# Norm tiles of x from TensorE transposes to column loads with repeated row numbers, in a cross-attention and FFN kernel

## The chip, the cores and the metric

One core of a Trainium2 chip runs the whole kernel. The metric is the device time in microseconds, the median of three runs. "The profile" is one execution taken by the hardware profiler; times in it count from the start of its span. Engines are PE (TensorE), DVE (VectorE), ACT (ScalarE), POOL (GpSimd) and SP (the engine that issues most DMAs).

## What is computed

```
x: (8, 256, 1024)   ctx: (8, 256, 1024)   32 query heads, 8 key/value heads, width 128
x = x + attention(layernorm(x), ctx, ctx, mask, wq, wk, wv, wo)
x = x + ffn(layernorm(x), qweight, lut4, bias)

layernorm(x) = (x - mean(x)) / sqrt(var(x) + 1e-5)      # over the last axis
attention: q = norm(x) @ wq, k = ctx @ wk, v = ctx @ wv, rotary positions on q and k,
           softmax(q k^T / sqrt(128) + mask) v, then @ wo
ffn:       y = norm(x) @ W^T + bias, W[o, i] = lut4[o, 4-bit code of (o, i)]
```

All arithmetic is float32. Each product is made of three passes over operands that are split in a high and a low part (`PASSES`).

## The kernel before, in words

The program is written out by hand for each engine; a semaphore stands for each hand-over, and each engine works strictly in the order of its own code. There are three stages.

**The key stage** (0 to 390 us of the profile) takes the eight batches one after the other (`batch(b)`, once per engine). On PE a batch is: eight key groups `g` (24 products of 256 columns each, L793) into two PSUM banks in turn, then four value products V0 to V3 (24 products of 512 columns each, L770) into two banks in turn, so that V2 needs the bank that V0 left and V3 the bank that V1 left. A bank is free when ACT has copied its high part and DVE has subtracted the low part (`values_high` L1089, `values_low` L1535). For each key group ACT swaps halves (L996, L997), DVE does cosine, sine and sum (L1372, L1381, L1387) and the low part (L1391), and SP stores it (L536). Between these DVE decodes the FFN weights of one output tile (`decode`, leaves L1568, picks L1575), and at the end it splits the context of the next batch (`context_low`, L1396), which the next batch's first key group needs. PE turns the decoded weights (L751).

**The query stage** (390 to 2160 us) has 256 units `u`, 6.86 us each, in rounds of 16 (`UNITS`): scores (L855), half or all of a query job (L839), attention times values (L896, odd units) and output projection (L925) on PE; mask, reciprocal, 32x32 transposes, splits and residual sums on DVE; exponents on ACT; normalization and query sines on POOL; 64 KB moves of the transposed probabilities on SP and ACT.

**The FFN stage** follows (L965).

**The norm tiles.** The queries need layernorm(x) with the model dimension on the partitions. x has sixteen tiles of 128 rows. Each is loaded with rows on partitions (`load_row`, L436, into `ln_row`), ACT takes the mean (`row_mean`, L1011), centres (`row_center`, L1017) and squares (`row_square`, L1026), DVE makes 1/sqrt (`row_var`, `row_scale`, L1404 to L1414), ACT scales the row (`row_norm`, L1035), PE turns the eight 128x128 blocks into PSUM (`turn_row`, L731, or `turn_side`, L870), ACT and DVE take high and low part out of PSUM into `raw` in two halves (`x_high` L1043, `x_low` L1422), and SP stores them to `x_scratch` (`store_row`, L443). Nine tiles pass in the key stage, in slots given by two tables: K slots (row work during the key groups, turned after V0) and V slots (row work during the values, turned after V3). Seven tiles pass in the query stage, one a round, at `ROW_AT` (u = 8 of a round), turned at u = 13 and 14 (`SIDE`). SP loads x back in `load_turned` (L449).

```
K_ROW = {1: 0, 2: 1, 3: 3, 4: 5, 5: 7, 6: 8}      # batch: tile
V_ROW = {2: 2, 3: 4, 4: 6}
ROW_AT = {UNITS * (e - A_ROWS) + 8: e for e in range(A_ROWS, NT)}
```

Of the kernel before, what the change touches and what calls it, by code (L numbers as in the profile page):

```python
# [14 lines left out]
def build_xattn_ffn(nc, x, ctx, mask, wq, wk, wv, wo, qweight, lut4, bias, x_rows, rope_cos, rope_sin, out):  # L15
# [138 lines left out]
    K_ROW = {1: 0, 2: 1, 3: 3, 4: 5, 5: 7, 6: 8}  # L154
    V_ROW = {2: 2, 3: 4, 4: 6}
# [5 lines left out]
    SIDE = {u + 5 + j: (e, j) for u, e in ROW_AT.items() for j in range(2)}  # L161
# [18 lines left out]
    x_scr = nc.dram_tensor("x_scratch", (NH, 2, C, P, 2, BANK), F32, kind="Internal").ap()  # L180
    res_scr = nc.dram_tensor("residual_scratch", (HT, P, D), F32, kind="Internal").ap()

    with ExitStack() as stack:
# [67 lines left out]
        x_mean, x_var0, x_var1, x_ve, x_sd, x_y, x_e, x_f, x_r = (stat_t[:, 56 + i:57 + i] for i in range(9))  # L251
# [34 lines left out]
        x_stored, res_stored, out_stored = sem("x_stored"), sem("res_stored"), sem("out_stored")  # L286
# [25 lines left out]
        row_ok, x_tr, x_hi, x_lo = sem("row_ok"), sem("x_tr"), sem("x_hi"), sem("x_lo")  # L312
# [45 lines left out]
        def rope_turns(j):  # L358

            return j - 1 if len(JOBS[j]) == 1 and (j == 0 or len(JOBS[j - 1]) == 1) else j  # L360

# [60 lines left out]
        def _(sp):  # L422
# [10 lines left out]
            def load_row(e):  # L433

                sp.wait_ge(x_tr, 2 * e)
                sp.dma_start(ln_row[:, :], x_tiles[e]).then_inc(row_in, 16)  # L436

            def store_row(e, j):

                sp.wait_ge(x_lo, 2 * e + j + 1)  # L440
                dst = x_scr[e // HT, e // REP % 2, 4 * j:4 * j + 4].rearrange("c p l (t n) -> t l p c n", n=P)
                for l in range(2):
                    done = sp.dma_start(dst[e % REP, l], raw_t[:, l * BANK:(l + 1) * BANK]  # L443
                                        .rearrange("p (c n) -> p c n", n=P))
                    done.then_inc(x_stored, 16)
# [58 lines left out]
            def batch(b, first=False, last=False):  # L504
# [14 lines left out]
                if last:  # L519
# [6 lines left out]
                    sp.wait_ge(x_tr, 2 * A_ROWS)  # L526
                    load_piece(wq[2], ln_row[:, :], a_raw_in[1])
                    sp.wait_ge(x_stored, 4 * 16 * A_ROWS)
# [3 lines left out]
                elif b - 1 in V_ROW:  # L532
                    load_row(K_ROW[b])
                for g in range(HKV):
# [13 lines left out]
                    elif not first:  # L548
                        if g == 0 and b - 1 in V_ROW:
                            store_row(V_ROW[b - 1], 0)  # L550
                        if g == TURN_AT[b]:
                            store_weights(b - 1, D0)
                        if g == 3 and b - 1 in V_ROW:
                            store_row(V_ROW[b - 1], 1)
# [27 lines left out]
                if first:  # L582
                    for t in range(TS):
                        load_context(1, t)
                    sp.wait_ge(w_lo, A_SLOTS + 2)
                    load_row(K_ROW[1])
                if b in V_ROW:
                    load_row(V_ROW[b])
                store_values(V0, 0, 0)
                sp.wait_ge(dq_step, b * DQ_STEPS + 1)  # L590
                load_planes(b + 1)
                if b in K_ROW:
                    store_row(K_ROW[b], 0)
                if b not in V_ROW and b in K_ROW and b + 1 in K_ROW:
                    load_row(K_ROW[b + 1])
                store_values(V1, 1, 0)
                if b in K_ROW:
                    store_row(K_ROW[b], 1)
                store_values(V2, 0, 1)
                store_values(V3, 1, 1)  # L600
# [24 lines left out]
            for u in range(NU):  # L625
# [9 lines left out]
                if u + 1 in PIECE and (u + 1) % UNITS not in LOAD_LAST:  # L635
                    if u - 1 in SIDE:
                        sp.wait_ge(x_stored, 4 * 16 * (SIDE[u - 1][0] + 1))
# [20 lines left out]
                if u in SIDE:  # L658
                    store_row(*SIDE[u])
# [4 lines left out]
                for j in range(2):  # L664
                    k = u - (HALF_UNITS - 14 + 8 * j)
                    if k == 1:
                        job = JOB_OF[HALF_UNITS - UNITS + 2 * REP * j + REP - 1]
                        sp.wait_ge(rope_mm, A_ROPES + job + 1)
                    for c in {1: (0, 1), 3: (2, 3), 5: (4, 5), 7: (6, 7)}.get(k, ()):
# [48 lines left out]
        def _(pe):  # L718
# [6 lines left out]

            def turn_row(e):

# [1292 lines left out]
```

## Time and profile before

| | us |
|---|---|
| median of 3 runs (lowest, highest) | 2340.43 (2339.54, 2340.71) |
| the profiled execution's own time | 2341.55 |
| its span | 2339.7 |
| PE busy, share of the span | 2327.5, 99% |
| DVE busy | 1691.2, 72% |
| ACT busy | 1116.5, 48% |
| POOL busy | 568.7, 24% |
| mean DMA rate | 140 GB/s |

Rows of the timeline give start, duration, engine, line, operation, tiles written and read, and in brackets the idle time before it with what ended it. Consecutive instructions of one engine overlap by some 0.1 us in these rows, so starts are used for distances. Rows of the chain of waits give start, duration and what the end of the program hung on. DMA rows give the median time from issue to landing.

### The profile page before, as it was taken

What the parts mean: (1) busy time and instruction counts of PE and PEld (TensorE: products, weight loads), DVE (VectorE), ACT (ScalarE), POOL (GpSimd) and SP (SyncE); (2) the same over time, 40 slices, a digit from 0 to 9 for tenths busy, and PEclk for the clock granted to TensorE, in tenths of its full rate; (3) what the DMA queues carried; (4) which work ended last, traced back from release to release, by engine and by line L of the source; (5) the groups of instructions that cost most, each with busy time, mean ns of one, the idle gap of its engine ahead of it and who ended that gap; (6) DMA issues with size and microseconds to landing.
All of it is one profiled execution on the core that took longest, in us unless ns stands there. A gap on an engine that the chain in (4) does not pass through costs nothing.

```text
span 2339.7 us, 35189 instructions
## 1 busy us (share of the span) xinstructions
PE 2327.5 (99%) x11902; PEld 1989.1 (85%) x11902; DVE 1691.2 (72%) x3811; ACT 1116.5 (48%) x2472; POOL 568.7 (24%) x675
## 2 busy tenths in 40 slices
PE   9999999999999999999999999999999999999999
PEld 8999999888888888888888888888888888888887
DVE  7888777667777777777777767677767776777773
ACT  5555544546464646455544444444444444444110
POOL 1000000332232323232233233323332332331320
PEclk9999999999999999999999999999999999999999
DMA  7466659544344343434456644333433333334442
GB/s 259 155 191 215 203 164 309 159 127 117 113 136 120 110 127 109 131 108 127 112 163 215 204 131 124 93 109 98 126 93 108 107 106 108 91 112 161 148 142 81
DMA packets 330098, 328.26 MB, mean 140 GB/s; under 512 B 32448, under 2 KB 266176, under 8 KB 329920
## 3 DMA queue, kind: packets, MB, share of 16 engines
q1 hardware_dynamic: 294496, 309.88, 43.0%
q10 hardware_dynamic: 35424, 16.14, 2.7%
q8 instruction: 95, 1.56, 0.3%
q14 instruction: 83, 0.68, 0.1%
HBM read 181.73 MB, written 71.30 MB: 108 GB/s over the span
## 4 chain that ended last, share of the span: by engine, by line
PE 94%; DVE 3%; DMA 1%; ACT 1%; issue 1%; POOL 0%; ACTq 0%; SPq 0%; POOLq 0%; DVEq 0%
PE bank L839 29%; PE bank L925 29%; PE bank L855 8%; PE bank L965 7%; PE bank L896 7%; PE bank L793 7%; PE bank L770 5%; DVE residual L1575 1%; DMA x_scratch<-raw 0%; DMA small_split<-probs 0%; POOL probs L1946 0%; DVE residual L1810 0%; DVE residual L1568 0%; PE bank L751 0%; PE bank L870 0%
## 5 line engine op out<-in xcount | busy, mean ns | idle before, releaser
L839 PE MATMUL bank<-acts_split,weights_split 128*128 128x512 f32 (+1 forms) x3192 | 742.9, 382 | 0.0
L925 PE MATMUL bank<-weights_split,small_split 128*128 128x512 f32 x3072 | 741.1, 390 | 1.6 <-DVE small_split L1794 1.6
L925 PEld LDWEIGHTS bank<-weights_split,small_split 128*128 128x128 f32 x3072 | 574.3, 188 | 121.4 <-DVE small_split L1794 2.6
L839 PEld LDWEIGHTS bank<-acts_split,weights_split 128*128 128x128 f32 x3192 | 576.5, 188 | 109.4
L1946 POOL TENSOR_SCALAR probs<-probs,row_numbers 128x256 f32<-128x256 f32 x512 | 358.0, 712 | 1191.1 <-DVE row_numbers L1780 1191.1
L1258 ACT ACTIVATE probs<-bank,row_numbers 128x256 f32<-128x256 f32 x512 | 238.1, 472 | 124.9 <-DVE row_numbers L1775 124.7
L1784 DVE STREAM_TRANSPOSE probs<-probs 128x512 f32<-128x512 f32 x250 | 177.6, 710 | 143.7 <-POOL probs L1946 143.7
L1938 POOL TENSOR_TENSOR rope_x<-rope_x,sin_t 128x512 f32<-128x512 f32 (+1 forms) x133 | 167.1, 1257 | 402.7 <-ACT rope_x L1231 402.6
L1769 DVE CUSTOM_DVE_ANT_0 bank<-bank,mask_tile 128x256 f32<-128x256 f32 x512 | 207.0, 445 | 65.2 <-PE bank L855 65.0
L1789 DVE TENSOR_TENSOR small_split<-small_split 128x512 fp32r<-128x512 f32 x250 | 179.2, 717 | 80.3 <-ACT small_split L1271 80.2
L855 PEld LDWEIGHTS bank<-small_split 128*128 128x128 f32 x1536 | 217.8, 190 | 21.0 <-DMA small_split<-k_scratch 1.0
L855 PE MATMUL bank<-small_split 128*128 128x256 f32 x1536 | 224.3, 282 | 0.5 <-DMA small_split<-k_scratch 0.5
L1284 ACT ACTIVATE small_split<-bank 128x512 fp32r<-128x512 f32 x127 | 75.8, 597 | 310.4 <-PE bank L896 310.4
L1271 ACT ACTIVATE small_split<-small_split 128x512 fp32r<-128x512 f32 x250 | 157.8, 631 | 119.8 <-DMA small_split<-probs 119.2
L896 PE MATMUL bank<-small_split 128*128 128x512 f32 x762 | 197.1, 394 | 1.7 <-issue 1.5
L793 PE MATMUL bank<-small_split,weights_split 128*128 128x256 f32 x1536 | 189.1, 285 | 3.0 <-issue 2.4
L793 PEld LDWEIGHTS bank<-small_split,weights_split 128*128 128x128 f32 x1536 | 186.7, 193 | 4.4 <-issue 3.8
L770 PE MATMUL bank<-acts_split,small_split 128*128 128x512 f32 x768 | 178.4, 391 | 0.1
L965 PE MATMUL bank<-weights_split,acts_split 128*128 128x512 f32 x768 | 174.5, 389 | 0.0
L965 PEld LDWEIGHTS bank<-weights_split,acts_split 128*128 128x128 f32 x768 | 144.1, 188 | 29.9
L770 PEld LDWEIGHTS bank<-acts_split,small_split 128*128 128x128 f32 x768 | 142.9, 188 | 29.8 <-DVE acts_split L1493 0.5
L1810 DVE TENSOR_TENSOR residual<-residual,bank 128x512 f32<-128x512 f32 x256 | 163.4, 679 | 0.0
(124 smaller groups left out, 2163.8 us busy)
## 6 DMA issues: line engine op xcount, KB each, us to landing
small_split<-probs SPq DMA_DIRECT2D x754, 64.0 KB, 2.2
raw<-in_L_xattn_wq SPq DMA_DIRECT2D x61, 512.0 KB, 3.9
raw<-in_L_xattn_wo SPq DMA_DIRECT2D x60, 512.0 KB, 3.8
k_scratch<-small_split SPq DMA_DIRECT2D x64, 256.0 KB, 2.3
v_scratch<-small_split SPq DMA_DIRECT2D x32, 512.0 KB, 2.9
x_scratch<-raw SPq DMA_DIRECT2D x64, 256.0 KB, 2.8
acts_split<-x_scratch SPq DMA_DIRECT2D x32, 512.0 KB, 5.4
mask_tile<-in_mask_BxSxS_ff SPq DMA_DIRECT2D x64, 256.0 KB, 2.9
```

Of the source, the lines that this page charges most:

```text
L770: done = pe.matmul(wide_ps[t][:, :], ctxT[:, c, a, t * P:(t + 1) * P], wv_s[:, c, m, n * BANK:(n + 1) * BANK], start=c == 0 and k == 0, st ...
L793: done = pe.matmul(k_ps[g % 2], wk_s[:, c, a, g * DK:(g + 1) * DK], ctxT[:, c, m, :], start=c == 0 and i == 0, stop=c == C - 1 and i == 2)
L839: last = pe.matmul(query_bank(j)[:, 0:wide], wq_s[:, h, c, a, :], xT[:, c, m, b * S:b * S + wide], start=c == 0 and i == 0, stop=c == C - ...
L855: last = pe.matmul(s_ps[:, t * S:(t + 1) * S], q_s[:, Q_SLOT[u], a, t * P:(t + 1) * P], k_s[:, m, :], start=i == 0, stop=i == 2)
L896: last = pe.matmul(o_ps[:, :], v_s[:, k, a, :], pT_keys[:, m, k], start=k == 0 and i == 0, stop=k == TS - 1 and i == 2)
L925: last = pe.matmul(out_ps[part][:, :], o_s[:, a, u % 2 * S + t * P:u % 2 * S + (t + 1) * P], wo_s[:, h, m, n * BANK:(n + 1) * BANK], start ...
L965: last = pe.matmul(out_ps[f % 2 * NN + n][:, :], xT[:, c, a, f % HT * P:(f % HT + 1) * P], w4_s[:, c, m, n * BANK:(n + 1) * BANK], start=c ...
L1258: last = act.activation(row, scored, ACT.Exp, bias=neg_max[:, u % 2, t:t + 1], accum_out=row_sum[:, u % 2, t:t + 1])
L1769: last = dve.tensor_tensor_reduce(out=s_ps[:, t * S:(t + 1) * S], in0=s_ps[:, t * S:(t + 1) * S], in1=mask_t[:, t, :], scale=1.0, scalar=- ...
L1784: dve.transpose(prob_rows[:, u % 2, :], prob_rows[:, u % 2, :]).then_inc(p_blocks, 1)
L1789: dve.tensor_tensor(pT_s[:, LO, u % 2, :], source, pT_s[:, HI, u % 2, :].bitcast(F32), ALU.subtract).then_inc(pT_lo, 1)
L1946: done = pool.tensor_scalar(row, row, row_inv[:, u % 2, t:t + 1], 1.0, ALU.mult, ALU.mult)
```

## The change

No norm tile is turned by PE any more. The row path stays up to 1/sqrt; `row_norm`, `turn_row`, `turn_side`, `x_high` and `x_low` are gone. Instead the host passes a second copy of x, `x_columns`, with the model dimension on the partitions. Per tile, SP stores minus the mean and 1/sqrt of the 128 rows to DRAM (`store_factors`, two words for each partition), loads them back repeated on all 128 partitions (`load_factors`), and loads the tile as columns (`load_columns`, 512 KB). DVE adds the mean and multiplies by the factor over 128x1024 (`columns_center`, `columns_scale`), ACT takes the high part in two halves (`columns_high`), DVE subtracts it (`columns_low`), SP stores both (`store_high`, two DMAs, and `store_low`, one). In the key stage the columns live in `raw`, in the query stage in `ln_row`. The slots in the key stage move by one batch: batch 1 has none, batch 5 gets a V slot; columns of a K slot are worked in the same batch's values, those of a V slot in the next batch's key groups. The sines of the keys are on DVE before and after.

```diff
-    K_ROW = {1: 0, 2: 1, 3: 3, 4: 5, 5: 7, 6: 8}
-    V_ROW = {2: 2, 3: 4, 4: 6}
+    K_ROW = {2: 0, 3: 2, 4: 4, 5: 6, 6: 8}
+    V_ROW = {2: 1, 3: 3, 4: 5, 5: 7}
...
-    SIDE = {u + 5 + j: (e, j) for u, e in ROW_AT.items() for j in range(2)}
+    COLS_AT = {u + 5: e for u, e in ROW_AT.items()}
...
+            def store_factors(e):
+
+                sp.wait_ge(row_r, e + 1)
+                sp.dma_start(fac_scr[e], x_factors).then_inc(factors_out, 16)
+
+            def load_columns(e):
+
+                if e >= A_ROWS:
+                    sp.wait_ge(row_step, 4 * e + 4)
+                elif e:
+                    sp.wait_ge(lo_stored, 16 * e)
+                else:
+                    sp.wait_ge(first_stored, 16)
+                sp.dma_start(cols_tile(e), x_columns[e]).then_inc(cols_in, 16)
+
+            def load_factors(e):
+
+                sp.wait_ge(factors_out, 16 * (e + 1))
+                sp.wait_ge(cols_step, 2 * e)
+                sp.dma_start(factors_t[:, :], fac_scr[e:e + 1].rearrange("a p k -> a (p k)").to_broadcast([P, 2 * P])
+                             ).then_inc(factors_in, 16)
...
-                if b in K_ROW:
-                    turn_row(K_ROW[b])
...
-                if u in SIDE:
-                    turn_side(u)
...
+            def columns_high(e):
+
+                act.wait_ge(cols_step, 2 * e + 2)
+                if e and e <= A_ROWS:
+                    act.wait_ge(hi_stored, 32 * e)
+                for j in range(2):
+                    done = act.activation(high_half(e, j), cols_half(e, j), ACT.Copy)
+                done.then_inc(cols_hi, 1)
...
+            def columns_center(e):
+
+                dve.wait_ge(cols_in, 16 * (e + 1))
+                dve.wait_ge(factors_in, 16 * (e + 1))
+                dve.tensor_tensor(cols_tile(e), cols_tile(e), factor(0), ALU.add).then_inc(cols_step, 1)
...
-                    if g == 0 and b - 1 in V_ROW:
-                        x_low(V_ROW[b - 1], 0, x_ps[0])
+                    if g == 2 and b - 1 in V_ROW:
+                        columns_center(V_ROW[b - 1])
                     if g == 3 and b - 1 in V_ROW:
-                        x_low(V_ROW[b - 1], 1, x_ps[1])
+                        columns_scale(V_ROW[b - 1])
+                    if g == 5 and b - 1 in V_ROW:
+                        columns_low(V_ROW[b - 1])
...
+                if u + 2 in COLS_AT:
+                    columns_center(COLS_AT[u + 2])
+                if u + 1 in COLS_AT:
+                    columns_scale(COLS_AT[u + 1])
+                if u - 1 in COLS_AT:
+                    columns_low(COLS_AT[u - 1])
```

The order of SP's DMAs in batch 4, from the key stores of groups 6 and 7 to the high part's store. L536 and L597 store keys, L454 and L513 load context, L436 and L466 load the row tile, L509 and L568 store values. Before:

```order
L536 DMA k_scratch<-small_split 128x512 [waits rope_lo] x2
L454 DMA residual<-in_ctx 128x1024 [waits ctx_lo]
L436 DMA ln_row<-in_x 128x1024 [waits x_tr]
L509 DMA v_scratch<-small_split 128x2x512 [waits stage_lo]
L457 DMA probs<-in_L_ffn_qweight 128x4x32 [waits dq_step]
L443 DMA x_scratch<-raw 128x4x128 [waits x_lo]
```

With the change:

```order
L597 DMA k_scratch<-small_split 128x512 [waits rope_lo]
L504 DMA x_scratch<-raw 128x8x128 [waits cols_lo]
L597 DMA k_scratch<-small_split 128x512 [waits rope_lo]
L471 DMA factor_scratch<-row_numbers 128x2 [waits row_r]
L481 DMA raw<-in_x_columns 128x1024 [waits lo_stored]
L513 DMA residual<-in_ctx 128x1024 [waits ctx_lo]
L466 DMA ln_row<-in_x 128x1024 [waits row_step]
L487 DMA column_factors<-factor_scratch 128x256 [waits cols_step,factors_out]
L568 DMA v_scratch<-small_split 128x2x512 [waits stage_lo]
L516 DMA probs<-in_L_ffn_qweight 128x4x32 [waits dq_step]
```

The low store of the V slot's tile (L504) comes after the key store of group 6; the columns of the K slot (L481) wait until it has landed; the factors (L487) are issued behind columns, context and row tile.

DVE in the same batch, from the low part of V0 to the first context split (L1535 and L1578 are the low parts of V0, V1, V2; L1575 and L1618 picks, L1568 and L1611 leaves of the decode). Before:

```order
L1535 TENSOR_TENSOR small_split<-bank,small_split 128x512 [waits stage_hi]
L1422 TENSOR_TENSOR raw<-bank,raw 128x512 [waits x_hi]
L1575 COPY_PREDICATED residual<-residual 128x1024 [waits dq_step]
L1568 TENSOR_SCALAR residual<-residual,probs 128x1024
L1568 TENSOR_SCALAR residual<-residual,probs 128x1024 [waits dq_step]
L1575 COPY_PREDICATED residual<-residual 128x1024 [waits dq_step]
L1535 TENSOR_TENSOR small_split<-bank,small_split 128x512 [waits stage_hi]
```

With the change:

```order
L1578 TENSOR_TENSOR small_split<-bank,small_split 128x512 [waits stage_hi]
L1455 TENSOR_TENSOR raw<-raw,column_factors 128x1024 [waits factors_in,cols_in]
L1618 COPY_PREDICATED residual<-residual 128x1024 [waits dq_step]
L1611 TENSOR_SCALAR residual<-residual,probs 128x1024
L1611 TENSOR_SCALAR residual<-residual,probs 128x1024 [waits dq_step]
L1618 COPY_PREDICATED residual<-residual 128x1024 [waits dq_step]
L1578 TENSOR_TENSOR small_split<-bank,small_split 128x512 [waits stage_hi]
L1459 TENSOR_TENSOR raw<-raw,column_factors 128x1024 [waits cols_step]
L1618 COPY_PREDICATED residual<-residual 128x1024 [waits dq_step] x2
L1445 TENSOR_SCALAR row_numbers<-row_numbers 128x1 [waits row_step]
L1464 TENSOR_TENSOR raw<-raw,mask_tile 128x512 [waits cols_hi]
L1464 TENSOR_TENSOR raw<-raw,small_split 128x512
```

Centring the columns (L1455) stands between the low part of V0 and the four decode steps ahead of V1's low part, and waits for both DMAs; scaling and low part stand between V1 and V2.

## Rows read from the trace of the kernel before

**Rows 1.** The page: busy time of the engines, share of the span, instructions

```profile
PE 2327.5 (99%) x11902; PEld 1989.1 (85%) x11902; DVE 1691.2 (72%) x3811; ACT 1116.5 (48%) x2472; POOL 568.7 (24%) x675
```

**Rows 2.** Chain of waits, PE in batch 4, then batch 6: start, us, what

```profile
199.03 5.75 PE bank L793 x48
...
222.92 5.47 PE bank L770 x24
...
229.26 16.34 PE bank L770 x72
245.61 0.87 PE bank L731 x8
246.48 5.75 PE bank L793 x48
...
293.05 5.75 PE bank L793 x48
...
339.63 0.87 PE bank L751 x8
```

**Rows 3.** The same view in one round of the query stage

```profile
576.63 2.75 PE bank L839 x12
...
590.35 2.75 PE bank L839 x12
...
618.76 2.75 PE bank L839 x12
```

**Rows 4.** Instructions by line: busy time and mean ns of one, idle time before

```profile
L1500 DVE TENSOR_TENSOR weights_split<-raw,weights_split 128x1024 fp32r<-128x1024 f32 x120 | 144.4, 1204 | 0.9 <-ACT weights_split L1332 0.8
...
L870 PE MATMUL bank<-ident,ln_row 128*128 128x128 f32 x56 | 8.4, 271 | 0.0
```

**Rows 5.** DVE in batch 4; then its window: PE, PEld, DVE, ACT, POOL, clock, DMA

```profile
224.85 0.42 DVE L1391 TENSOR_TENSOR small_split<-rope_a,small_split 128x256 fp32r<-128x256 f32 x1
...
229.70 0.71 DVE L1535 TENSOR_TENSOR small_split<-bank,small_split 128x512 fp32r<-128x512 f32 x1
...
230.90 1.33 DVE L1575 COPY_PREDICATED residual<-residual 128x1024 f32<-128x1024 uint8 x1
...
236.73 0.69 DVE L1535 TENSOR_TENSOR small_split<-bank,small_split 128x512 fp32r<-128x512 f32 x1 [1.71 <-ACT small_split L1089]
...
239.39 2.69 DVE L1575 COPY_PREDICATED residual<-residual 128x1024 f32<-128x1024 uint8 x2
...
205.65:253.11 47.46, 47.46 (x315) 43.57 (x314) 37.33 (x82) 26.86 (x57) 0.00 (x0) 1.00 0.65 202
```

**Rows 6.** DMA from 228 to 236 us, issue to landing; then a window's busy time, share, GB/s

```profile
ln_row<-in_x SPq DMA_DIRECT2D x1, 512.0 KB, 5.7
...
probs<-in_L_ffn_qweight SPq DMA_DIRECT2D x1, 64.0 KB, 5.7
...
222.00:236.00 14.00, 14.00 (x71) 11.80 (x70) 12.88 (x23) 4.66 (x8) 0.00 (x0) 1.00 0.94 279
```

**Rows 7.** DMA of the whole program, median us from issue to landing

```profile
raw<-in_L_xattn_wq SPq DMA_DIRECT2D x61, 512.0 KB, 3.9
...
w_scratch<-small_split SPq DMA_DIRECT2D x14, 512.0 KB, 3.7
```

**Rows 8.** Timeline: keys of batches 2 and 3 start on PE; batch 2's last key store on SP

```profile
102.74 11.75 PE L793 MATMUL bank<-small_split,weights_split 128*128 128x256 f32 x96 [0.33 <-DVE small_split L1396]
...
151.33 5.99 PE L793 MATMUL bank<-small_split,weights_split 128*128 128x256 f32 x48 [0.24 <-DVE small_split L1396]
...
132.39 0.58 SPq L536 DMA_DIRECT2D k_scratch<-small_split  x1
```

**Rows 9.** Timeline of DVE and PE in the query stage, one round's units 12 and 13

```profile
594.23 0.76 DVE L1789 TENSOR_TENSOR small_split<-small_split 128x512 fp32r<-128x512 f32 x1 [0.35 <-ACT small_split L1271]
...
598.59 0.69 DVE L1794 TENSOR_TENSOR small_split<-bank,small_split 128x512 fp32r<-128x512 f32 x1 [0.94 <-ACT small_split L1284]
...
596.37 1.55 PE L896 MATMUL bank<-small_split 128*128 128x512 f32 x6
...
600.84 3.02 PE L925 MATMUL bank<-weights_split,small_split 128*128 128x512 f32 x12
```

More of the change, by code:

```diff
@@ L360, in rope_turns, with cols_home, cols_tile, cols_half @@
             return j - 1 if len(JOBS[j]) == 1 and (j == 0 or len(JOBS[j - 1]) == 1) else j
+        def cols_home(e):
+            return raw if e < A_ROWS else ln_row[:, :]
+        def cols_tile(e):
+            return cols_home(e).rearrange("p (c n) -> p c n", c=C)
+        def cols_half(e, j):
+            return cols_home(e)[:, j * BANK:(j + 1) * BANK]
+        def high_half(e, j):
+            if e < A_ROWS:
+                return (mask_t[:, :, :].rearrange("p t k -> p (t k)").bitcast(F32R), R[:, 4096:4608])[j]
+            return x_split_all[:, j * BANK:(j + 1) * BANK]
+        def factor(i):
+            return factors_t[:, :].rearrange("p (a n k) -> p k a n", a=1, k=2)[:, i].to_broadcast([P, C, P])
         def query_bank(j):
@@ L591, in batch @@
                 load_planes(b + 1)
-                if b in K_ROW:
-                    store_row(K_ROW[b], 0)
-                if b not in V_ROW and b in K_ROW and b + 1 in K_ROW:
+                if b == 1:
                     load_row(K_ROW[b + 1])
@@ L724, in _ @@
                 pe.transpose(x_ps[1][:, 0:P], ident[:, :], ident[:, :])
-            def turn_row(e):
-                pe.wait_ge(row_ok, e + 1)
-                pe.wait_ge(x_lo, 2 * e)
-                for c in range(C):
-                    last = pe.transpose(x_ps[c // 4][:, (c % 4) * P:(c % 4 + 1) * P],
-                                        ln_row[:, c * P:(c + 1) * P], ident[:, :])
-                    if c % 4 == 3:
-                        last.then_inc(x_tr, 1)
             def turn_rows(f):
@@ L829, in query @@
                             pe.wait_ge(row_step, 4 * ROW_AT[squares + 1] + 4)
-                    for rows in (u for u, side in SIDE.items() if u < units[0] and side[1] == 0):
-                        if WORK[rows + 1][0][0] == j:
-                            pe.wait_ge(x_lo, 2 * SIDE[rows][0] + 1)
-                        if WORK[rows + 3][0][0] == j:
-                            pe.wait_ge(x_lo, 2 * SIDE[rows][0] + 2)
                 for c in chunks:
@@ L1709, in batch @@
                 if b in K_ROW:
[L1710 removed]
+                    columns_center(K_ROW[b])
                 for k in range(end - 4 if b in OWN else end - 5, end - 1):
```

158 lines of the change are left out of this document (82 added, 76 removed).

## The prediction

> **What bounds the kernel now.** I read the page first [rows 1]: PE is busy 2327.5 us, 99% of the span, at a granted clock of 1.00 (2.4 GHz) in the windows read [rows 5, 6], so any work taken from PE counts at once, as long as nothing else becomes late. Then the chain of waits in order of time. In a batch of the key stage [rows 2] PE pieces follow each other without a hole: batch 4 runs from 199.03 to 246.48, 47.45 us, with two norm tiles in it, batch 6 from 293.05 to 339.63, 46.58 us, with one. The difference, 0.87, is one turned tile. In the query stage [rows 3] a pair of units takes 13.72 us (576.63 to 590.35), and the two pairs in which a tile is turned take 28.41 (590.35 to 618.76), 0.97 more than 27.44. Last the timelines of DVE and of the DMA queue where the new work goes [rows 5 to 7]. There DVE is busy 37.33 of 47.46 us of a batch, and between 222 and 236 us the DMA engines are 94% busy.
>
> **What PE sheds.** 128 transposes. Nine tiles of the key stage at 0.87 and seven of the query stage at 0.97: 7.8 + 6.8 = 14.6 us, if PE is never made to wait. The record of one transpose says 271 ns [rows 4], yet eight cost 0.87 us on the path, because they overlap; the path price is the one for the sum. The Trainium skill, "TensorE: Matmul & The Clock Gate", Part 4, gives about 275 ns for a 128x128 transpose inside a kernel. The record agrees with it; a sum by it would be 128 times 0.275, 35 us, an estimate that the 0.87 of the chain rules out.
>
> **What DVE gets.** Per tile two passes over 128x1024. The nearest row is another 128x1024 product of two tensors, 1204 ns [rows 4], 2.4 us a tile. The low parts are 2 times 512 columns as before. A batch with two tiles then needs 37.3 + 4.8 = 42.1 us of DVE, and without turned tiles PE wants to be through in 47.45 - 1.74 = 45.7. That leaves 3.6 us of idle time in a batch for everything DVE must wait for.
>
> **The chain behind the K slot's columns, on the clock of batch 4.** Centring, scaling and the low part in groups 2, 3 and 5 take 3.6 us where 1.2 stood before; about 0.8 fits in holes, and DVE reaches the low part of group 6 near 226.4 and that of V0 near 231.3, 1.6 later than its 224.85 and 229.70 [rows 5]. That alone delays no product: V0's bank is wanted at 233.9. But one thing now hangs on another:
>
> 1. SP stores the low columns of the V slot's tile behind the key store of group 6, near 227.1. A 512 KB store in 512-byte pieces lands 3.7 us after its issue [rows 7]. In a full queue it is later: 2.1 MB issued from 223.6 on (keys, high part, context, keys, low part) at 279 GB/s [rows 6] are 7.5 us, so 231 to 232. I take 232, since the engines are 94% busy there.
> 2. SP waits for that, then issues the columns of the K slot (both use `raw`), context, row tile, factors, in this order. A 512 KB load alone lands after 3.9 us [rows 7]: 235.9. Each further 512 KB is 1.9 us at 279 GB/s, the repeated factors (128 KB) 0.5: context 237.8, row tile 239.7, factors 240.2. I take 240.
> 3. DVE sits in front of `columns_center` from 232 to 240. Behind it in its order are pick, two leaves and pick, 4.0 us from 230.90 until the next low part could start, and V1's low part, 0.6: 240 + 1.2 + 4.0 + 0.6 = 245.8. V3 needs it, and PE would be there at 229.26 - 0.87 + 10.9 = 239.3 [rows 2]. PE waits 6.5 us.
> 4. From V1's low part to the next batch's keys DVE has scaling 1.2, two picks 2.6 (the pair at 239.39 [rows 5]), the row's variance 0.2, low columns 1.2, factor steps 0.9, V2's low part 0.6 and the first context split 0.6: 7.3 us, more than V3's 5.5. The next keys start at 253.1. The batch takes 54.1 us in place of 47.45: **6.6 longer**.
>
> The same path by batch. Batches 3 and 4: 6.6 each. Batch 5 had one tile and 46.6 us, now two: 7.5. Batch 6 has no V slot, so no row tile ahead of the factors (1.9 less) and no row numbers after: 4. Batch 2 has no low store to wait for, its columns go out after the last key store at 132.39 [rows 8], the factors land near 142.5 (four loads behind a full queue), V1's low part is done at 142.5 + 1.2 + 2.8 + 0.6 = 147.1, the next keys start 7.3 later at 154.4 in place of 151.3 [rows 8]: 3. Batch 1 loses its tile and the 0.33 us that PE waited for the context after it [rows 8]: -1.2. Batches 0 and 7 do the same work as before; batch 7 waits for the stored tiles much as it did, and I cost that at nothing: batch 6's store is hidden under seven microseconds of decode and values, and costs up to 3 if that cover is gone. Sum of the key stage: -1.2 + 3 + 6.6 + 6.6 + 7.5 + 4 = **+26.5 us**.
>
> **The query stage.** There is room. SP issues columns and factors in unit 10, a unit before DVE centres them at the end of unit 11, and the 4.4 MB more over this stage's 1770 us are nothing against 279 GB/s. ACT loses `row_norm`. DVE's two passes go behind the cosine of unit 11 and the transposes of unit 12 and push what follows by 1.2 and 1.9 us. Two hand-overs come close: the low part of unit 11's probabilities, at 594.23 now, ends near 596.1, and the attention product that reads it starts at 596.37; the low part of the output, at 598.59, ends near 600.05, and the projection starts at 600.84, 0.44 earlier without the turn [rows 9]. Both hold by 0.1 to 0.4 us. I take the full gain, 7 times 0.97, **-6.8 us**, with 0 to 3 us lost as the other bound. The stores of the factors in 8-byte pieces have no row of their own; nearest are small loads, and their cost is in the chain above only if they take over 11 us (issue 229, wanted with the rest at 240), so nothing. The key sines stay where they were: nothing.
>
> **The sum.** +26.5 - 6.8 = +19.7 on the profiled execution's own 2341.55: 2361. The median of the runs is 1.1 lower: **2360 us**, 0.8% slower. Bounds: step 1 at its best (3.7 after issue, 230.8) and step 2 with nothing queued would give the quick rivals below; step 2 with every load 1 us later adds some 5 us.
>
> **Rivals.**
>
> A. *The queue keeps up* (faster). The place is `columns_center` of the K slots: if the factors have landed when DVE comes from V0's low part (231.3), DVE's 42.1 us fit almost in 45.7 and PE gets 8 to 14.6 us: 2326 to 2332. It decides at about 235.8: there the five batches lose 1.4 each and the 6.8 of the query stage is used up. For it speaks that reads and writes might overlap better than 279 GB/s. Against it speaks that even an unloaded queue gives 227.1 + 3.7 + 3.9 = 234.7 for the columns alone.
>
> B. *The factors overtake the big loads.* Then DVE starts with the columns at 236. ACT still takes the row tile's mean before V1's high part: 239.7 + 1.2 + 0.6, V1's low part at 242.1, the next keys at 249.4. Batches 3 and 4 lose 2.9, batch 5 3.8, batches 2 and 6 together 3: 12.4 with batch 1, less 6.8: +5.6, 2346. Against it: 64 KB of code planes, issued 1.5 us behind the row tile, took 5.7 us to land, as the row tile did [rows 6]; they kept their place. The Trainium skill, "DMA: Bandwidth & Descriptors", section on queues, rings and completion order, says that each DMA engine takes descriptors in ring order but that a later one may finish its write before an earlier one; the first half agrees with the 5.7, the second no row here shows.
>
> C. *The query stage stalls too.* If the hand-overs of units 12 and 13 are 1 us late in each of seven rounds, 7 us of the gain go and the key stage's loss may be larger as well: 2367 to 2375.
>
> D. *A and B mixed*: the factors are in time in some batches and not in others, and loss and gain cancel within 5 us, 2336 to 2345.
>
> **How the numbers follow.** Forecast (2350 to 2368) 0.58; A 0.15; B (2341 to 2350) 0.14; C 0.07; D (2336 to 2345) 0.06. A measurement of this kernel can tell about 0.2%, 4.7 us, from no change. Faster by more: A and a little of D, 0.16. Within: most of D and a little of B, 0.06. Slower: the rest, 0.78. The range leaves out A and half of C: 2335 to 2371. The forecast's own range is 2350 to 2368.
>
> **What would show it.** In the profile after: DVE idle for 6 to 8 us ahead of `columns_center` in batches 3 to 5, released by the DMA of the factors; PE waiting for V1's low part and for the context's low part, 4 to 7 us a batch; periods of 54 us from key group 0 to key group 0; rounds of the query stage 0.97 us shorter with hardly a wait. Wrong would be: keys starting every 46 us (A); PE waits for the probabilities' low part in units 12 to 13 (C).

## The result, and the profile after

| | before | after |
|---|---|---|
| median of five runs each (lowest to highest), us | 2340.43 (2339.54 to 2345.84) | 2384.36 (2382.17 to 2386.72) |
| span of the profiled execution, us | 2339.7 | 2382.6 |

The ratio is 1.0182, with a 95% interval of 1.0171 to 1.0193: slower by 44 us, where 20 were forecast. That is 16 us above the forecast's own range (2350 to 2368) and 13 above the wider one (2335 to 2371).

The busy line of the page, which answers to [rows 1]:

```profile
PE 2328.8 (98%) x11774; PEld 1984.0 (83%) x11774; DVE 1721.2 (72%) x3843; ACT 1101.7 (46%) x2456; POOL 563.0 (24%) x675
```

PE has 128 instructions less, and yet is busy 1.3 us longer, in a span that is 42.9 longer. The values explain both: first by line, before and after, with busy time, mean ns and the idle time before them; then in the waits of PE in the key stage, 60 to 400 us (total, times, longest):

```profile
L770 PE MATMUL bank<-acts_split,small_split 128*128 128x512 f32 x768 | 178.4, 391 | 0.1
```

```profile
L836 PE MATMUL bank<-acts_split,small_split 128*128 128x512 f32 x768 | 188.4, 407 | 41.0 <-DVE small_split L1578 40.9
```

```profile
PE bank L836 <- DVE small_split L1578: 40.9, 5, 9.6
```

The five waits all stand before V3, for V1's low part, in batches 2 to 6. PE's timeline in batch 4 (start, us, what, and in brackets the idle time before; it answers to [rows 2]), with V3 of batches 2, 3 and 6:

```profile
145.11 8.05 PE L836 MATMUL bank<-acts_split,small_split 128*128 128x512 f32 x24 [5.19 <-DVE small_split L1578]
...
203.71 7.78 PE L836 MATMUL bank<-acts_split,small_split 128*128 128x512 f32 x24 [9.37 <-DVE small_split L1578]
...
211.32 5.92 PE L859 MATMUL bank<-small_split,weights_split 128*128 128x256 f32 x48
...
224.62 12.70 PE L859 MATMUL bank<-small_split,weights_split 128*128 128x256 f32 x96 [0.76 <-DVE rope_a L1403]
237.16 16.51 PE L836 MATMUL bank<-acts_split,small_split 128*128 128x512 f32 x72
262.39 7.47 PE L836 MATMUL bank<-acts_split,small_split 128*128 128x512 f32 x24 [8.73 <-DVE small_split L1578]
269.70 5.92 PE L859 MATMUL bank<-small_split,weights_split 128*128 128x256 f32 x48
...
378.13 7.64 PE L836 MATMUL bank<-acts_split,small_split 128*128 128x512 f32 x24 [9.56 <-DVE small_split L1578]
```

The reader is to see three things. The batch lasts 58.4 us (211.32 to 269.70) in place of 47.45. The wait for V1's low part is 8.7 of it. And V3, 24 products, takes 7.5 to 8.2 us behind such a wait, where 24 products are 5.5 us of the chain in [rows 2].

What held V1's low part is in DVE's and ACT's timelines of the same batch, and what held these in SP's:

```profile
256.58 1.23 DVE L1455 TENSOR_TENSOR raw<-raw,column_factors 128x1024 f32<-128x1024 f32 x1 [10.43 <-DMA column_factors<-factor_scratch]
...
261.66 0.68 DVE L1578 TENSOR_TENSOR small_split<-bank,small_split 128x512 fp32r<-128x512 f32 x1
...
256.17 1.06 ACT L1054 ACTIVATE ln_row<-ln_row 128x1024 f32<-128x1024 f32 x1 [12.75 <-DMA ln_row<-in_x]
...
257.23 0.58 ACT L1129 ACTIVATE small_split<-bank 128x512 fp32r<-128x512 f32 x1
```

```profile
241.41 0.43 SPq L504 DMA_DIRECT2D x_scratch<-raw  x1
...
243.30 1.22 SPq L471 DMA_DIRECT2D factor_scratch<-row_numbers  x1
248.05 0.33 SPq L481 DMA_DIRECT2D raw<-in_x_columns  x1
248.43 0.43 SPq L513 DMA_DIRECT2D residual<-in_ctx  x1
248.91 0.43 SPq L466 DMA_DIRECT2D ln_row<-in_x  x1
250.70 0.33 SPq L487 DMA_DIRECT2D column_factors<-factor_scratch  x1
```

And the DMAs issued in these ten microseconds, with the time from issue to landing:

```profile
x_scratch<-raw SPq DMA_DIRECT2D x1, 512.0 KB, 6.6
raw<-in_x_columns SPq DMA_DIRECT2D x1, 512.0 KB, 5.5
...
ln_row<-in_x SPq DMA_DIRECT2D x1, 512.0 KB, 7.2
column_factors<-factor_scratch SPq DMA_DIRECT2D x1, 128.0 KB, 5.8
factor_scratch<-row_numbers SPq DMA_DIRECT2D x1, 1.0 KB, 7.4
```

Two chains leave SP and meet in V1's low part. **DVE's:** the store of the row numbers, issued at 243.30, lands 7.4 us later; only then does SP issue the load that repeats them (250.70), which takes 5.8; DVE stands in `columns_center` until 256.5. In this batch the chain of waits goes through exactly these two DMAs. **ACT's:** SP stands before the columns until the low store has landed (248.0), so the row tile, third behind it, is issued at 248.91 and lands at 256.1; ACT stands in `row_mean`, and V1's high part is behind it. The two releases come 0.4 us apart, but they are not equally far from V1's low part: ACT's high part of V1 is done at 257.8, while DVE has the centring, a pick, two leaves and a pick before it and reaches V1's low part at 261.66. DVE's chain is the longer one by 3.9 us.

The whole key stage ends 46.1 us later (first query job at 432.4 for 386.3), and the rest gives back 3.2. The parts of the 46.1: waits before V3 40.9; V3's longer products 11.0 (39.1 in five batches, less five times the 5.63 that V3 took before); late key groups 4.8; nine turns saved -7.8; the rest, some -3, mostly in batches 0 and 1.

The late key groups have a cause of their own in SP's order. At the end of a batch SP loads the V slot's columns into `raw`, waits for that until the K slot's low store has landed, and V3's values are stored only behind it. Between batches 3 and 4 the chain of waits shows both DMAs, and ACT's timeline the end of it:

```profile
208.70 6.73 DMA x_scratch<-raw
...
215.84 5.54 DMA v_scratch<-small_split
```

```profile
221.40 0.42 ACT L1042 ACTIVATE small_split<-rope_a 128x256 fp32r<-128x256 f32 x1 [3.29 <-DMA v_scratch<-small_split]
```

So batch 4's key groups are late from the start, and with them its own stores.

### The profile page after: what moved, and what is told of

Same layout as the page of the kernel before. It is cut to its first block, busy times and chain, and to the rows that moved or that the text cites. A ratio compares the mean times of both kernels' runs of the same rounds, so it can differ in the third digit from the quotient of the medians.

```text
span 2382.6 us, 34975 instructions
## 1 busy us (share of the span) xinstructions
PE 2328.8 (98%) x11774; PEld 1984.0 (83%) x11774; DVE 1721.2 (72%) x3843; ACT 1101.7 (46%) x2456; POOL 563.0 (24%) x675
## 4 chain that ended last, share of the span: by engine, by line
PE 85%; DVE 6%; DMA 6%; issue 1%; ACT 1%; POOL 0%; SPq 0%; ACTq 0%; DVEq 0%
PE bank L896 28%; PE bank L968 28%; PE bank L913 7%; PE bank L1006 7%; PE bank L939 7%; PE bank L836 4%; PE bank L859 4%; DMA column_factors<-factor_scratch 1%; DMA factor_scratch<-row_numbers 1%; DVE residual L1618 1%; DMA small_split<-probs 1%; DMA x_scratch<-raw 1%; DVE residual L1611 1%; DMA v_scratch<-small_split 1%; POOL probs L1997 0%
## 5 line engine op out<-in xcount | busy, mean ns | idle before, releaser
L1997 POOL TENSOR_SCALAR probs<-probs,row_numbers 128x256 f32<-128x256 f32 x512 | 352.8, 701 | 1200.9 <-DVE row_numbers L1827 1200.9
L836 PE MATMUL bank<-acts_split,small_split 128*128 128x512 f32 x768 | 188.4, 407 | 41.0 <-DVE small_split L1578 40.9
L836 PEld LDWEIGHTS bank<-acts_split,small_split 128*128 128x128 f32 x768 | 150.6, 198 | 75.6 <-DVE small_split L1578 43.0
```

What stands on the lines that cost most here:

```text
L836: done = pe.matmul(wide_ps[t][:, :], ctxT[:, c, a, t * P:(t + 1) * P], wv_s[:, c, m, n * BANK:(n + 1) * BANK], start=c == 0 and k == 0, st ...
L1997: done = pool.tensor_scalar(row, row, row_inv[:, u % 2, t:t + 1], 1.0, ALU.mult, ALU.mult)
```

## Experiments

My theory after the trace: the two chains cost the time, DVE's own work little. The rivals: DVE's added passes; one chain alone; something in the query stage. All rows on PE's waits below cover the key stage, up to 440 us at most.

### Where: key stage or query stage

`queries_columns` turns the nine tiles of the key stage by PE as before; `keys_columns` does the opposite.

```diff
+    # queries_columns: key stage as before the change
+                if b in K_ROW:
+                    turn_row(K_ROW[b])
+    # keys_columns: query stage as before the change
+                if u in SIDE:
+                    turn_side(u)
```

Expected of the first:

> Full computation: the nine tiles of the key stage go through the row tile and TensorE as in the kernel before, the seven of the query stage are loaded as columns as in the changed one. My theory (the 44 us all come from DVE's and ACT's waits in the key stage): 2340 less the 6.8 of seven turns plus the 3.6 that the changed kernel's query stage gave back, so 2337 (2333 to 2340). Rival (the query stage's columns cost as well, through DMA and DVE work): 2342 or more.

Measured: 2338.0 us, ratio 0.9986 (0.9977 to 0.9996). Expected of the second:

> Full computation, the mirror: nine tiles of the key stage as columns as in the changed kernel, the seven of the query stage turned by TensorE as before. My theory: the whole loss is here, 2384 + 3.2 = 2387 (2384 to 2391), with TensorE's waits before V3 of 5 to 10 us in each of batches 2 to 6 as in the changed kernel. Rival (a share of the loss is the query stage's): 2375 or less.

Measured: 2398.7 us, 1.0244 (1.0223 to 1.0266). PE's waits before V3 are the changed kernel's:

```profile
PE bank L839 <- DVE small_split L1622: 38.1, 5, 8.8
```

The loss is the key stage's; the query stage's columns are worth 1 to 5 us. The second is 12 us more than expected. Its key stage ends 46.1 us late, as in the changed kernel; the excess is in the query stage, 7 us of it in units 112 to 144, where PE waits up to 2.8 us for DVE's low part of the probabilities, whose transfers come late. Why they do so in this mixture alone stays open.

### Which slot

`v_slots` has columns only for the V slots (and the query stage), `k_slots` only for the K slots.

```diff
+    COLUMNS = set(range(A_ROWS, NB * TS)) | set(V_ROW.values())    # v_slots
+    COLUMNS = set(range(A_ROWS, NB * TS)) | set(K_ROW.values())    # k_slots
```

> Full computation: columns for the V slots of the key stage (tiles 1, 3, 5, 7) and for the query stage; the K slots (0, 2, 4, 6, 8) are turned by TensorE as before. My theory (only what stands ahead of V1's low part costs; a V slot's passes lie in the keys of the next batch, far behind their transfers): no waits before V3, four turns less, keys up to 0.5 us late a batch: 2340.5 - 3.5 - 3.2 + 1.5 = 2335 (2331 to 2341). Rival (any columns in the key stage cost through their 5 to 7 us transfers and DVE's passes): 2350 or more.

Measured: 2336.4 us, 0.9987 (0.9975 to 0.9998). Its longest sum of PE waits in the key stage (four of them):

```profile
PE bank L911 <- DVE small_split L1512: 3.6, 4, 1.5
```

> Full computation, the other half: columns for the K slots, the V slots turned by TensorE. The columns' buffer is free early, and neither the factor store nor the row tile stands behind the store of a V slot's low part. My theory (row numbers at 241.6 in batch 4, store of the factors 6.1, load of the factors 5.7, centring, V1's low part: about 2 to 3 us earlier than with both): waits before V3 of 5 to 7 us in each of batches 2 to 6, 2368 (2358 to 2376). Rival (the buffer shared by two tiles a batch is the cause, not the factors' way through DRAM): 2345 or less.

Measured: 2368.7 us, 1.0116 (1.0102 to 1.0129), with waits before V3 of 3.0 to 5.1 us. In batch 4 of `k_slots` the row numbers are stored at 236.83, with no low store ahead, and land in 3.6 us; the load goes out at once:

```profile
236.83 0.43 SPq L493 DMA_DIRECT2D factor_scratch<-row_numbers  x1
...
240.40 0.33 SPq L509 DMA_DIRECT2D column_factors<-factor_scratch  x1
...
246.38 1.23 DVE L1545 TENSOR_TENSOR raw<-raw,column_factors 128x1024 f32<-128x1024 f32 x1 [6.69 <-DMA column_factors<-factor_scratch]
```

So the K slots alone cost 27 us, with the columns' buffer free early: the factors' way through DRAM is enough for that. The V slots alone, whose factors have half a batch of time, cost nothing, and their key groups are not late although DVE's two passes stand in them: the last 144 products of the keys take 17.5 to 17.6 us in batches 3 to 6, as before the change, for 18.1 to 19.5 with both kinds. The end of the key stage, against before, is 25.3 us later with the K slots alone, 1.8 earlier with the V slots alone and 46.1 later with both. Even when the 3.2 us that batches 0 and 1 gain are counted only once, some 20 us come only when both kinds share `raw` and the queue.

### Two chains side by side

`row_first` loads the row tile ahead of the factor store and the columns. `centre_late` moves DVE's centring and scaling behind V1's low part and the last picks. `both_moved` does both.

```diff
                         if g == HKV - 1 and b in K_ROW:
+                            if b in V_ROW:
+                                load_row(V_ROW[b])          # row_first
                             store_factors(K_ROW[b])
                             load_columns(K_ROW[b])
...
-                if b in K_ROW:
-                    columns_center(K_ROW[b])               # centre_late
                 for k in range(end - 4 if b in OWN else end - 5, end - 1):
                     decode(b, k)
                 values_low(V1)
-                if b in K_ROW:
-                    columns_scale(K_ROW[b])
                 for k in range(end - 1, end + 1):
                     decode(b, k)
+                if b in K_ROW:
+                    columns_center(K_ROW[b])
+                    columns_scale(K_ROW[b])
```

> Full computation: the changed kernel, but the row tile of the V slot is loaded ahead of the factor store and the columns instead of behind them, in batches 2 to 4 (batch 5 too). My theory (two chains of equal length, DVE's centring behind the factor store and load, ACT's mean behind the row tile): the factor chain still holds DVE to about 256.5 us in batch 4, so less than 2 us a batch are won, 2378 to 2384. Rival (the row tile alone binds, DVE's centring only looks late): the waits before V3 fall by 8 us in four batches and the clock stays up, 2340 to 2350.

Measured: 2387.0 us, 1.0195 (1.0171 to 1.0219). ACT now begins at 252.05, DVE still at 256.80:

```profile
256.80 1.23 DVE L1455 TENSOR_TENSOR raw<-raw,column_factors 128x1024 f32<-128x1024 f32 x1 [9.78 <-DMA column_factors<-factor_scratch]
```

> Full computation: the changed kernel, but DVE centres and scales the K slot's columns behind V1's low part and the last picks, instead of centring ahead of them. My theory: DVE no longer passes the factor chain on to V1's low, but in batches 2 to 5 ACT still waits for the row tile until about 256.2 us before V1's high part, so V1's low comes about 3 us earlier there (about 258.5 for 261.7 in batch 4) and on time in batch 6, which has no V slot: 12 us there and 3 to 5 in each of the others, 2356 (2350 to 2365). Rival 1 (DVE's added passes cost the time, wherever they stand): 2378 to 2384, next keys late instead of V3. Rival 2 (the factor chain alone binds): 2335 to 2342.

Measured: 2385.3 us, 1.0184 (1.0164 to 1.0205), a miss by 29 us. The waits before V3 for V1's low part do halve, but what they give comes back elsewhere: the next keys wait for the context's low part and for late cosines, and ACT is still held by the row tile:

```profile
PE bank L836 <- DVE small_split L1578: 20.4, 4, 6.6
PE bank L859 <- DVE small_split L1427: 6.2, 4, 2.2
PE bank L859 <- DVE rope_a L1403: 5.9, 4, 2.4
PE bank L836 <- DVE small_split L1427: 4.4, 1, 4.4
```

```profile
259.33 1.06 ACT L1054 ACTIVATE ln_row<-ln_row 128x1024 f32<-128x1024 f32 x1 [13.46 <-DMA ln_row<-in_x]
```

> Full computation: the row tile first and DVE's centring and scaling behind V1's low part, the two edits together that gave nothing alone. My theory (two waits side by side, ACT for the row tile and DVE for the factors, either of which holds V1's low part to about 261 us): now V1's low part comes on time and V3 starts without a wait, but the factors still arrive at 256.6 us, so V2's low part and the context's low parts, which stand behind the columns on DVE, end at about 264, when the next keys should start at 259: about 5 us a batch of the 9.4 stay, and some of the clock's 2.2: 2362 (2350 to 2372). Rival 1 (nothing but the two waits): 2335 to 2342. Rival 2 (DVE's passes cost the time wherever they stand): 2378 to 2386.

Measured: 2360.1 us, 1.0088 (1.0068 to 1.0108).

```profile
PE bank L859 <- DVE small_split L1427: 14.4, 4, 4.1
...
PE bank L836 <- DVE small_split L1578: 0.3, 1, 0.3
```

Two edits that each give nothing give 24 us together: V1's low part was held twice, first by DVE's chain and, 3.9 us under it in batch 4, by ACT's. What stays is the wait named in advance, at the next keys (L1427), since the factors come no earlier, and 3.5 us for late cosines.

### The transfers or DVE's work

`dve_only` keeps all of DVE's and ACT's work on the columns, but leaves out the loads of columns and factors in the key stage. DVE then waits itself for the store of the last low part, which SP waited for before the columns.

```diff
             def load_columns(e):
+                if e < A_ROWS:
+                    return
             def load_factors(e):
+                if e < A_ROWS:
+                    return
...
             def columns_center(e):
...
+                elif e:
+                    dve.wait_ge(lo_stored, 16 * e)
```

> Leaves out the loads of the columns and of the factors for the nine tiles of the key stage (their centring, scaling, high and low parts are computed from what the buffers hold, and stored); DVE's and ACT's instructions, the factor stores and all other transfers stay. My theory (the wait for transfers, not DVE's added work, is what costs): TensorE's 41 us before V3 go, the clock's 11 with them, most of the 5 of late keys stay: 2332 (2325 to 2345). Rival (DVE's two more passes a tile make V1's low part late by themselves): 2365 or more, with waits before V3 of 5 us or more.

Measured: 2348.8 us, 1.0031 (1.0016 to 1.0046), 17 us over my number and outside its range, though far from the rival's. PE's waits:

```profile
PE bank L841 <- DVE small_split L1589: 7.3, 4, 2.3
PE bank L864 <- DVE small_split L1432: 5.5, 4, 1.4
```

The end of the key stage comes 7.4 us later than before the change, for 46.1 in the changed kernel. So at least 38.7 us are the transfers', with what follows from their waits. The other 15.2 (7.4 and the 7.8 of the turns) are not all DVE's passes. The 7.3 us before V3 all lie in batches 3 to 6, where DVE still waits for the low store, 9.5 us in these four; in batch 4:

```profile
235.55 1.23 DVE L1466 TENSOR_TENSOR raw<-raw,column_factors 128x1024 f32<-128x1024 f32 x1 [3.15 <-DMA x_scratch<-raw]
```

Batch 2 has no such store ahead and no wait before V3. DVE's own are the 5.5 us before the next keys, 1.4 in each of batches 2 to 5; 2.4 us are not assigned.

`factors_given` takes one leg of DVE's chain away: the K slots' factors are read from a fixed part of x, with no wait for the store, and the row tile goes first.

```diff
+                given = e < A_ROWS and e in K_ROW.values()
+                if not given:
+                    sp.wait_ge(factors_out, 16 * (e + 1))
```

> Leaves out the use of the row's own mean and scale for the five K slots of the key stage: their factors are read from a fixed part of x, ahead of the columns, with no wait for the factor store; the row tile is loaded first as well. The columns are then DVE's last wait. My theory (store of the low part, columns, and beside them row numbers, store of the factors, load of the factors; the second ends 3 us behind the first): the centring starts at the columns' landing, 253.5 instead of 256.6 in batch 4: 3 us a batch, 2369 (2362 to 2375), and the waits before V3 are 5 to 7 us. Rival 1 (the round trip of the factors is the whole chain): 2345 or less. Rival 2 (it is no limit at all): 2380 or more.

Measured: 2371.6 us, 1.0136 (1.0119 to 1.0153), waits before V3 of 4.0 to 6.7 us. DVE is now released by the columns, issued behind the low store's landing:

```profile
248.93 1.22 DVE L1456 TENSOR_TENSOR raw<-raw,column_factors 128x1024 f32<-128x1024 f32 x1 [5.70 <-DMA raw<-in_x_columns]
```

So the columns behind the shared buffer are a second leg, which holds PE nearly as long: without the factors' round trip the time falls by 12.8 us, 2.6 a batch, and no more.

### The clock

`fill` puts 36 to 80 turns of the identity into a free bank between V2 and V3 of batches 2 to 6, so that PE is busy while it waits.

```diff
                 values(2)
+                for _ in range(FILL.get(b, 0)):
+                    pe.transpose(w4_ps[0][:, 0:P], ident[:, :], ident[:, :])
                 values(3)
```

> Full computation: the changed kernel with 36, 80, 76, 70 and 80 turns of the identity into a free bank between V2 and V3 of batches 2 to 6, so that TensorE is busy while it waits for V1's low part. My theory (the 2.2 us that V3 takes longer is the granted clock that falls with the idle time before it): the wait is as long as before, filled with turns of 0.1 us, and V3's last 24 products take 5.6 us instead of 7.5 to 8.2: 11 us less, 2373 (2369 to 2378). Rival (V3 is slower for another reason, such as its weight loads or the late bank): no change, 2382 to 2387.

Measured: 2381.2 us, 1.0179 (1.0158 to 1.0200). In batch 4:

```profile
252.39 8.46 PE L875 MATMUL bank<-ident 128*128 128x128 f32 x76
261.37 5.74 PE L837 MATMUL bank<-acts_split,small_split 128*128 128x512 f32 x24 [0.53 <-DVE small_split L1581]
268.47 1.78 PE L860 MATMUL bank<-small_split,weights_split 128*128 128x256 f32 x13 [1.36 <-DVE small_split L1430]
```

and the windows of V3, changed kernel first, then this one (us, busy PE, PEld, DVE, ACT, POOL, granted clock, DMA share, GB/s):

```profile
262.30:270.20 7.90, 7.81 (x29) 6.36 (x30) 7.76 (x15) 3.81 (x8) 0.00 (x0) 0.76 0.64 201
```

```profile
261.30:267.20 5.90, 5.74 (x24) 4.43 (x24) 5.76 (x12) 3.16 (x7) 0.00 (x0) 1.00 0.54 178
```

Shown: V3 is slow because part of it runs at 1.2 GHz after the wait (granted clock 0.50 from 256 to 262 us in the changed kernel, on average 0.76 in V3's window), and at 2.4 GHz it takes 5.74 us. What this is worth in the time is a miss: I expected 11 us. The median is 3 us lower, but the interval of its ratio contains that of the changed kernel, so the runs show no gain; in the two traces the key stage ends 3.5 us earlier, 2.0 of it in batch 6, where no next keys wait for the context. In the others, with V3 quick, the next keys wait 1.4 us for the context's low part, which DVE cannot give sooner. The clock term overlaps the next wait. The Trainium skill, "TensorE: Matmul & The Clock Gate", Part 1, says that the array falls back to half its clock when it has been idle; these windows agree.

### Attempts at a better kernel

`pool_keys` gives centring and scaling in the key stage to POOL, idle there, puts a K slot's high and low parts into the next batch and orders SP's queue anew.

```diff
+            for e in range(A_ROWS):
+                pool.wait_ge(cols_in, 16 * (e + 1))
+                pool.wait_ge(factors_in, 16 * (e + 1))
+                pool.tensor_tensor(cols_tile(e), cols_tile(e), factor(0), ALU.add).then_inc(cols_step, 1)
+                pool.wait_ge(cols_step, 2 * e + 1)
+                pool.tensor_tensor(cols_tile(e), cols_tile(e), factor(1), ALU.mult).then_inc(cols_step, 1)
```

> Full computation: in the key stage POOL, idle there, centres and scales the columns; a K slot's high and low parts are made in the next batch (keys 1 and 2) instead of between the values, a V slot's ahead of V0's; the row tile is loaded at the last keys, and no wait for a store of a low part stands ahead of it. My theory (the loss is the two waits for transfers that DVE and ACT pass on to V1's low part, and some DVE work): none of them is left, TensorE does nine turns less than before at 0.87 us and the query stage gives 3.2 us: 2340.5 - 7.8 - 3.2 = 2330 (2326 to 2338), POOL's two passes 2.5 us each by the 1.25 us of its 128x512 product. Rival 1 (POOL's passes slow DVE's beside them, or take far longer): 2340 to 2350. Rival 2 (the transfers themselves, 1 MB a tile more in the key stage, cost): 2345 or more, with waits for planes, context or stores.

Measured: 2365.5 us, 1.0101 (1.0083 to 1.0119). New waits took the old ones' place, the longest on ACT and DVE: ACT for the factor store before it may overwrite the mean (20.3 us in four waits), for POOL (14.9 in four) and for key stores (23.8 in eleven). One pass of POOL and the DVE instruction beside it:

```profile
235.56 2.48 POOL L1985 TENSOR_TENSOR raw<-raw,column_factors 128x1024 f32<-128x1024 f32 x1
235.69 3.60 DVE L1621 COPY_PREDICATED residual<-residual 128x1024 f32<-128x1024 uint8 x1
```

The same pick takes 1.33 us at 231.89. `v_pool` is `v_slots` with POOL's passes for its four tiles and nothing else, to see this alone.

> Full computation: v_slots (columns for the V slots of the key stage and for the query stage, K slots turned by TensorE) with the V slots' centring and scaling on POOL instead of DVE. My theory (in v_slots DVE's two passes of 1.22 us a batch are what is left: TensorE waits 0.3 to 1.5 us for the context's low parts at the next keys, 4 us in all with 0.46 before V3): these waits go, 2336.4 - 3.5 = 2333 (2330 to 2337), POOL's passes 2.4 to 3.9 us each as in pool_keys and ready before ACT's high parts. Rival (DVE's passes beside POOL's get slower by as much, or the waits are another's): 2336 or more.

Measured: 2345.5 us, 1.0021 (1.0012 to 1.0030), 9 us worse than `v_slots`. Again the rival:

```profile
208.57 2.43 POOL L2084 TENSOR_TENSOR raw<-raw,column_factors 128x1024 f32<-128x1024 f32 x1
...
208.78 2.51 DVE L1497 TENSOR_TENSOR rope_x<-rope_x,sin_t 128x256 f32<-128x256 f32 x1
```

A product of DVE that takes 0.42 elsewhere ends 0.3 us after POOL's pass: DVE stood still for it. The Trainium skill, "SBUF — State Buffer", section on who interferes with whom, says that a DVE instruction with two inputs in SBUF and a GpSimd one that reads SBUF exclude each other, the later one waiting in full. The two rows agree.

## Why the prediction was wrong

The direction, the place (`columns_center` of the K slots, released by the factors; V1's low part; PE before V3) and the query stage's sign were right; the size was not: 44 us for 20. Batch 4's clock of before is the one of after less 12.3 (it starts at 211.32 for the 199.03 of [rows 2]).

What failed is the time at which the factors land, in two terms: the landing of the low store in step 1 was set too early, and the store of the factors in step 2 was set at nothing. Both stand in the chain of waits of the changed kernel, here in batch 3 and in batch 6:

```profile
183.93 7.43 DMA factor_scratch<-row_numbers
191.38 6.43 DMA column_factors<-factor_scratch
...
356.62 9.23 DMA x_scratch<-raw
...
366.79 5.44 DMA column_factors<-factor_scratch
```

- **PE sheds 14.6 us.** Right on the path: 0.97 less in the two pairs of each round, as steps of 0.49 and 0.48.
- **Step 1**, low store issued 227.1, landed 232. In batch 4 it was issued at 229.1 and landed at 235.7, 6.6 us after its issue for the 4.9 taken. The 2.0 us of late issue are the late key groups above, which my sum did not have: I let the buffer hold SP once a batch, and it does so twice. Counted from the start of each batch, the landing was forecast at 33.0 and came at 34.1, 36.7, 35.1 and 39.0 in batches 3 to 6, 13.1 us too late in all.
- **Step 2.** I let the factors wait in line behind columns, context and row tile, 0.5 us for their bytes, and costed their store at nothing unless it took over 11 us from 229. In place of that stands a round trip of its own: store issued at 231.0, load issued 238.4, landed 244.2. The bound was wrong in kind: SP does not issue the load until the store has landed, so both latencies add. Past the wait for the low store, this held SP another 2.9, 1.3 and 1.4 us in batches 3 to 5. In batch 6 it held nothing, since the low store took 9.2 us and landed, within 0.3 us, when the row numbers did.
- **Steps 1 and 2 together** put the factors at 244.2 for 240 in batch 4. From the start of the batch they were forecast at 41.0, and at 39.1 in batch 6; they landed at 44.8, 45.2, 43.2 and 45.4. Batch 6 has the largest error, a loss of 12.2 (58.8 for 46.6) for the 4 forecast. 6.3 of it are the factors' landing and nearly all the rest V3's low clock.
- **Step 3**, V1's low part done at 245.8, PE waits 6.5: 250.0 and 8.7. Picks and leaves behind the centring took the 4 us I gave them.
- **Step 4**, next keys 7.3 us after V1's low part: 7.4 (262.3 to 269.7). Here PE came last, because V3 was slow. The clock after an idle engine was not in my sum. It adds little while DVE's 7.3 us run beside it: 3 to 4 us over five batches in the traces, 1.8 of them in batch 6.
- **By batch**: forecast 54.1 for 3, 4 and 5; measured 58.3, 58.4 and 57.1. Batch 2: 53.5 for 51.7. Batches 0 and 1 together gained 3.2 for the 1.2 forecast.
- **The query stage**: -6.8 forecast with 0 to 3 lost; -3.2 measured (with the FFN stage), so 3.6 lost. It is not rival C: in units 12 and 13, where C had the stall, each round shed its 0.97. The loss is in other units, where scores come later by steps of 0.2 to 0.9 us. What causes them stays open.
- **Rival B** (factors overtake, the row tile binds ACT) had half of it: ACT's chain is real and, in batch 4, 3.9 us shorter than DVE's. My text had them as alternatives; they hold side by side, which `row_first`, `centre_late` and `both_moved` show. B's sum has a slip besides: its terms add to 11.4 and not 12.4. And where A decides, 235.8 gives 2.4 us a batch by steps 3 and 4, not 1.4.
- **The range** took in no case in which two waits stand in one batch or the round trip is serial; its upper end came from a 1 us shift per load.

`v_slots` (2336.4) and `queries_columns` (2338.0) are both faster than the kernel before and after. Against the one before it is 0.13 to 0.14%, with intervals that end just short of 1, under what I called measurable; the two don't differ from each other.

## What to carry to other kernels

Where a value goes to DRAM and comes back, count store and load as two full latencies in a row, each behind whatever the queue has just been given, even for a kilobyte; place the round trip where half a stage lies between its ends. Before moving a wait away, list every engine that stands between it and the late result, since taking away one of two chains that end close together gives little or nothing (0 us for either here, 24 for both). Where a buffer is used twice a period, look at both places in which its store holds the queue. And an idle POOL is no free help where DVE is nearly full.

## What I had not expected of the hardware

- A 1 KB store of row numbers takes 3.6 us to land behind key stores only (`k_slots`), 4.2 (median) in the query stage, and 6.1 (median) in the key stage, 7.4 behind a 512 KB store. The 128 KB load back takes 4.1 in the query stage, 5.7 in the key stage (medians).
- Behind a wait of 5 to 10 us of PE 24 products take 7.5 to 8.2 us in place of 5.6, in batch 4 at a mean granted clock of 0.76 in that stretch.
- POOL's 128x1024 product of two tensors takes 2.43 us, and DVE instructions beside it last until it ends: 2.51 us for a product of 0.42, 3.60 for a pick of 1.33.
